# A fused two-layer graph kernel: the node pass's first six steps placed between the second edge stage's last groups

## What is computed

```python
h = relu(layernorm(x))
x = x + L0(h)     # edge messages (q*k*dk attention), summed by dst, times Wo, plus h
h = relu(layernorm(x))
x = x + L1(h)
# L1: deg = 1 + segment_sum(edge_weight, src); dinv = rsqrt(deg)
#     agg[i] = sum over edges src=i of dinv[i]*w*dinv[dst]*h[dst]  +  dinv[i]^2 * h[i]
#     out = relu(agg @ (W @ W1) + (b @ W1 + b1)) @ W2 + b2
```

## Time and profile before

| | before |
|---|---|
| median of 3 runs | 1825.09 us (1824.55 to 1827.22) |
| the profiled execution: its time | 1813.87 us |
| the profiled execution: span from first to last instruction | 1812.2 us |
| mean granted TensorE clock over the span | 0.943 |
| PE busy | 1607.8 us (89%) |
| DVE busy | 1424.0 us (79%) |
| POOL busy | 1214.8 us (67%) |
| ACT busy | 1127.9 us (62%) |

### The profile page before, as it was taken

One profiled execution on the slowest core, in us unless ns is written; L12 is line 12 of the kernel. 1 busy time (PEld: TensorE's weight loads), 2 busy tenths in 40 slices (PEclk: granted clock), 3 DMA queues, 4 the chain that ended last, 5 costly groups with the idle time before them and its releaser, 6 DMA issues.

```text
span 1812.2 us, 29106 instructions
## 1 busy us (share of the span) xinstructions
PE 1607.8 (89%) x6406; PEld 1097.8 (61%) x6406; DVE 1424.0 (79%) x5625; ACT 1127.9 (62%) x2142; POOL 1214.8 (67%) x864
## 2 busy tenths in 40 slices
PE   6999999999999927677675099999999999999998
PEld 3556666666666615455553066677666666666776
DVE  8887877777777539888785788888888888888873
ACT  2345566666666402222222398889998889888884
POOL 5325888888887457888887766666666666666650
PEclk9999999999999968888887599999999999999999
DMA  9999666666666736656655889999999999999971
GB/s 373 417 416 342 158 188 195 191 183 184 184 192 194 206 73 117 116 127 112 128 110 107 201 222 268 265 272 271 266 272 265 273 264 271 267 264 270 274 223 77
DMA packets 148029, 398.73 MB, mean 220 GB/s; under 512 B 20144, under 2 KB 56756, under 8 KB 147974
## 3 DMA queue, kind: packets, MB, share of 16 engines
q1 hardware_dynamic: 88038, 278.61, 44.5%
q0 software_dynamic: 56416, 115.46, 33.8%
q10 hardware_dynamic: 3520, 4.07, 0.7%
HBM read 217.84 MB, written 180.23 MB: 220 GB/s over the span
## 4 chain that ended last, share of the span: by engine, by line
PE 53%; POOL 20%; DMA 11%; DVE 9%; issue 6%; SPq 1%; ACT 0%; POOLq 0%; DVEq 0%; ACTq 0%
PE bank L1394 11%; PE bank L1383 11%; POOL sums_dram L504 9%; PE bank L1278 8%; DMA out_dram<-cg 6%; PE bank L1271 4%; PE bank L1285 4%; PE bank L1320 4%; POOL kept L601 4%; POOL cg L508 4%; POOL b_rs L500 3%; PE bank L1373 3%; DMA sums_dram<-ub,sidx 2%; PE bank L1259 2%; DVE cg L995 2%
## 5 line engine op out<-in xcount | busy, mean ns | idle before, releaser
L1394 PE MATMUL bank<-w_sb,kept 128*128 128x256 f32 x1568 | 354.3, 379 | 0.0
L1383 PE MATMUL bank<-kept,w 128*128 128x512 f32 x784 | 353.3, 593 | 0.0
L601 POOL TENSOR_TENSOR kept<-kept 128x1024 f32<-128x1024 f32 x98 | 232.3, 2370 | 177.1 <-DVE cg L995 177.1
L1394 PEld LDWEIGHTS bank<-w_sb,kept 128*128 128x128 f32 x1568 | 298.1, 190 | 81.7 <-issue 46.3
L1347 PE MATMUL bank<-cg,en 128*128 128x256 f32 x386 | 130.4, 482 | 121.7 <-ACT cg L1148 67.1
L500 POOL TENSOR_TENSOR b_rs<-b_ve,minus_half 128x8 f32<-128x8 f32 x102 | 210.3, 2062 | 28.2 <-DVE b_ve L1012 28.2
L1383 PEld LDWEIGHTS bank<-kept,w 128*128 128x128 f32 x784 | 141.8, 191 | 140.9 <-issue 140.9
L1186 ACT ACTIVATE kept<-kept,b_nb,b_rs 128x256 f32<-128x256 f32 x392 | 202.2, 588 | 22.0 <-DVE b_nb L985 22.0
L1176 ACT ACTIVATE kept<-kept,b_nb,b_rs 128x256 f32<-128x256 f32 x392 | 202.3, 589 | 10.2 <-DVE b_nb L985 10.2
L504 POOL DMA_INDIRECT sums_dram<-ub,sidx x96 | 156.2, 1627 | 53.8 <-issue 27.0
L1347 PEld LDWEIGHTS bank<-cg,en 128*128 128x128 f32 x386 | 93.0, 248 | 153.8 <-issue 136.7
(11 more groups left out here) (179 smaller groups left out, 3355.8 us busy)
## 6 DMA issues: line engine op xcount, KB each, us to landing
sums_dram<-cg SPq DMA_DIRECT2D x196, 512.0 KB, 15.2
kept<-in_x_dram SPq DMA_DIRECT2D x97, 512.0 KB, 6.0
kept<-sums_dram POOLq DMA_DIRECT2D x97, 512.0 KB, 10.0
cg<-sums_dram SPq DMA_DIRECT2D x97, 512.0 KB, 8.5
out_dram<-cg SPq DMA_DIRECT2D x97, 512.0 KB, 10.0
row_k<-keys_dram SPq DMA_DIRECT2D x24, 256.0 KB, 4.5
row_s<-in_src_dram SPq DMA_DIRECT2D x24, 256.0 KB, 4.3
row_d<-in_dst_dram SPq DMA_DIRECT2D x41, 128.0 KB, 3.9
```

The source lines that it names most:

```text
L601: pool.tensor_tensor(X1[k.slot(8)], X[k.slot(4)], H[k.slot(2)], ALU.add).then_inc(g_xh, 1)
L1383: ins = pe.matmul(bank[:, 2 + m, :], w01[:, c, m * P:(m + 1) * P], hT[k.slot(2)][:, c * GN:(c + 1) * GN], start=(c == 0), stop=(c == KC - 1))
L1394: ins = pe.matmul(to, rT[k.slot(2)][:, c * GN + j * P:c * GN + (j + 1) * P], w2_sb[:, c, :], start=False, stop=(c == KC - 1), skip_group_c ...
```

## The change

`AHEAD` becomes 6. VectorE, ScalarE and SP run `messages2` (SP: its row loads) for steps 0 to 11 as before (`first_quads`: four in line, eight in a loop), then 12 to 26 in line, and behind steps 13, 15, 17, 19, 21 and 23 they run node steps 0 to 5. POOL, all in line, runs node steps 0 to 5 behind its steps 14, 16, 18, 20, 22 and 24 (`lag=1`). PE has nothing to do in these node steps and runs `messages2(25)` and then node step 6 on.

In the first six node steps the sum X1 = X + H, which occurs in steps 2 to 5, is done on VectorE in four instructions of 128x256 instead of on POOL in one of 128x1024; POOL keeps the accumulating DMA and the power. The buffers over `kept` are ordered X, H, X1, H1, AG, hT, rT. Instead of one wait for 22 groups, SP waits for 4 groups ahead of its first X load, VectorE for the group over which each X1 lies (7 to 10) and, ahead of the first AG, for 18. SP's node step 6 loads X(6) and then S1(0) and S1(1), the first after the wait for all scatters. The memset of b_mv on VectorE comes behind step 11. All that follows node step 5 is as before.

```diff
@@ -26,7 +26,9 @@
 Q = 4
 NQ = -(-EC // Q)
 SPARE = ROWS - N
-AHEAD = 5
+AHEAD = 6
+FRONT_FROM = 12
+FRONT_AT = (13, 15, 17, 19, 21, 23)
 HOT_STEPS = (10, 8, 8, 8, 11, 11, 11, 11, 10, 10)
 HOT_RING = 6
 SCATTER_LAG = 9
@@ -302,10 +304,16 @@
             return place(late, [P, width])
 
         X = [part(G * D) for _ in range(4)]
-        X1 = [part(G * D) for _ in range(8)]
+        x_rooms = late[0] // (Q * D)
         H = [part(G * D) for _ in range(2)]
+        X1, x1_rooms = [], []
+        for _ in range(8):
+            X1.append(part(G * D))
+            x1_rooms.append(late[0] // (Q * D))
         H1 = [part(G * D) for _ in range(2)]
         AG = [part(G * D) for _ in range(2)]
+        ag_rooms = late[0] // (Q * D)
+        assert G == Q and ag_rooms <= NQ - 2
         hT = [part(KC * GN) for _ in range(2)]
         rT = [part(KC * GN) for _ in range(2)]
         ROOMS = -(-late[0] // D)
@@ -347,14 +355,21 @@
 
             return t[(slice(None), bass.ds(k.value(0, Q), chunks(k)), *i)]
 
-        def last_quads(messages2, nodes):
-
-            for i in range(AHEAD):
-                if i == 0:
-                    messages2(Step(NQ))
-                if i == 2:
-                    messages2(Step(NQ + 1))
-                nodes(Step(i))
+        def first_quads(eng, messages2):
+
+            for p in range(4):
+                messages2(Step(p))
+            with eng.Fori(1, FRONT_FROM // 4) as reg:
+                for u in range(4):
+                    messages2(Step(u, reg, 4))
+
+        def last_quads(messages2, nodes, since=FRONT_FROM, lag=0):
+
+            for p in range(since, NQ + 2):
+                messages2(Step(p))
+                for i in range(AHEAD):
+                    if FRONT_AT[i] + lag == p:
+                        nodes(Step(i))
 
         def load_pair(eng, k):
 
@@ -433,10 +448,8 @@
                                  src[bass.ds(k.value(0, Q * P), wide)].rearrange("(a e) -> a e", a=1)
                                  .broadcast_to([P, wide])).then_inc(n_row[k.slot(2)], 16)
 
-            run_steps(sp, NQ, 0, 4, 4, load_src)
-
-
-            sp.wait_ge(n_h, ROOMS // Q)
+            first_quads(sp, load_src)
+
             STORE = NODE_STEPS + 1
 
             def nodes(s):
@@ -445,17 +458,20 @@
                     if k.past(4):
 
                         pass_on(sp, (g_xh, k.value(-3)))
+                    elif not k.past(1):
+                        sp.wait_ge(n_h, x_rooms)
                     sp.dma_start(X[k.slot(4)][0:parts_of(k), :], group(x, k, parts_of(k))
                                  ).then_inc(g_x[k.slot(4)], 16)
-                k = s.back(5)
-                if k.within(NG):
-                    if not k.past(1):
-
-                        sp.wait_ge(n_sc, 16 * EC)
-                    if k.past(4):
-                        pass_on(sp, (g_ag, k.value(-3)))
-                    sp.dma_start(S1[k.slot(4)][0:parts_of(k), :], group(sums1, k, parts_of(k))
-                                 ).then_inc(g_s1[k.slot(4)], 16)
+                if s.past(AHEAD):
+                    for k in [s.back(5)] if s.past(AHEAD + 1) else [Step(0), Step(1)]:
+                        if k.within(NG):
+                            if not k.past(1):
+
+                                sp.wait_ge(n_sc, 16 * EC)
+                            if k.past(4):
+                                pass_on(sp, (g_ag, k.value(-3)))
+                            sp.dma_start(S1[k.slot(4)][0:parts_of(k), :], group(sums1, k, parts_of(k))
+                                         ).then_inc(g_s1[k.slot(4)], 16)
                 k = s.back(STORE)
                 if k.within(NG):
 
@@ -463,7 +479,8 @@
                     sp.dma_start(group(out, k, parts_of(k)), OUT[k.slot(2)][0:parts_of(k), :]
                                  ).then_inc(g_out[k.slot(2)], 16)
 
-            run_steps(sp, NG, STORE + 1, 8, 4, nodes)
+            last_quads(load_src, nodes)
+            run_steps(sp, NG, STORE + 1, 8, 4, nodes, start=AHEAD)
             for q in range(2):
                 sp.wait_ge(g_out[q], 16 * ((NG - q + 1) // 2))
 
@@ -587,18 +604,16 @@
                     for i in range(chunks(Step(k))):
                         scatter_add(sums1, sidx2[k % 4][:, i:i + 1], UB2[k % 2][i // 2][:, i % 2, :], last_row1, n_sc)
 
-            for p in range(NQ):
-                messages2(Step(p))
-
             def nodes(s):
                 k = s.back(2)
                 if k.within(NG):
 
-                    pass_on(pool, (g_h, k.value(1)))
-                    if k.past(8):
-
-                        pass_on(pool, (g_fin, k.value(-7)))
-                    pool.tensor_tensor(X1[k.slot(8)], X[k.slot(4)], H[k.slot(2)], ALU.add).then_inc(g_xh, 1)
+                    if s.past(AHEAD):
+                        pass_on(pool, (g_h, k.value(1)))
+                        if k.past(8):
+
+                            pass_on(pool, (g_fin, k.value(-7)))
+                        pool.tensor_tensor(X1[k.slot(8)], X[k.slot(4)], H[k.slot(2)], ALU.add).then_inc(g_xh, 1)
                     pass_on(pool, (g_xh, k.value(1)))
                     pool.dma_start(X1[k.slot(8)][0:parts_of(k), :], group(sums0, k, parts_of(k)),
                                    accum_op=ALU.add).then_inc(g_s0[k.slot(4)], 16)
@@ -609,7 +624,7 @@
                         pool.wait_ge(g_h1, k.value(-5))
                     inv_sqrt(b_ve[k.slot(2)][:, :, :], b_rs[k.slot(2)][:, :, :], g_ve, g_rs, k)
 
-            last_quads(messages2, nodes)
+            last_quads(messages2, nodes, since=0, lag=1)
             run_steps(pool, NG, NODE_STEPS, 8, 4, nodes, start=AHEAD)
 
 
@@ -966,7 +981,7 @@
                     dve.scalar_tensor_tensor(nb[q][:, 0:n, :], mv[q][:, 0:n, 0:1], -1.0, rs[q][:, 0:n, :], ALU.mult,
                                              ALU.mult).then_inc(n_nb, 1)
 
-            run_steps(dve, NQ, 0, 4, 4, messages2)
+            first_quads(dve, messages2)
 
             for i in range(2):
 
@@ -975,6 +990,16 @@
             def nodes(s):
                 a, v, r, t = s, s.back(1), s.back(5), s.back(4)
                 z = v.slot(2)
+                k = s.back(2)
+                if k.within(NG) and not s.past(AHEAD):
+
+                    dve.wait_ge(n_h, x1_rooms[k.slot(8)])
+                    dve.wait_ge(g_h, k.value(1))
+                    for j in range(G):
+                        at0 = slice(j * D, (j + 1) * D)
+                        ins = dve.tensor_tensor(X1[k.slot(8)][:, at0], X[k.slot(4)][:, at0], H[k.slot(2)][:, at0],
+                                                ALU.add)
+                    ins.then_inc(g_xh, 1)
                 if v.within(NG + 4):
                     dve.wait_ge(g_rs, v.value(1))
                     if r.within(NG):
@@ -1016,6 +1041,8 @@
                     dve.wait_ge(g_h1, k.value(1))
                     if k.past(2):
                         dve.wait_ge(g_T, k.value(-1))
+                    elif not k.past(1):
+                        dve.wait_ge(n_h, ag_rooms)
 
                     dve.wait_ge(g_s1[k.slot(4)], k.turns(4))
                     for j in range(G):
@@ -1156,7 +1183,7 @@
                         ins = act.activation(UB2[q][i].rearrange("p i d -> p (i d)"), bank[:, 6 * q + i, :], ACT.Copy)
                     ins.then_inc(n_UB, 1)
 
-            run_steps(act, NQ, 0, 4, 4, messages2)
+            first_quads(act, messages2)
 
             def nodes(s):
                 k = s.back(7)
@@ -1361,7 +1388,7 @@
                 ins.then_inc(g_bits, 1)
 
             def nodes(s):
-                if s.reg is None and s.off == AHEAD - 1:
+                if s.reg is None and s.off == AHEAD:
                     open_banks()
                 k = s.back(7)
                 if k.within(NG):
@@ -1395,7 +1422,7 @@
                                             start=False, stop=(c == KC - 1), skip_group_check=True)
                     ins.then_inc(g_m2, 1)
 
-            last_quads(messages2, nodes)
+            messages2(Step(NQ))
             run_steps(pe, NG, NODE_STEPS, 8, 4, nodes, start=AHEAD)
 
 
```

## The result

The changed kernel takes 1816.41 us (median of 5 runs, 1815.92 to 1819.55) against 1825.09 of before: ratio 0.9957, 95% interval 0.9942 to 0.9972. It is faster by 7.8 us by the ratio, 8.7 by the medians; 16.0 were forecast. The time lies inside the range and the sign is right, but the gain is about half of the forecast, so the sum is wrong somewhere.

The account below looks back on a forecast made before the run. POOL was taken to bound the edge stage, TensorE the node pass. With +15.5, -2.3 and -2.6 to the last scatter and a shorter way on, PE's full step moves from 1048.5 to 1032.5: 1825.1 - 16.0 = 1809.1 us, range 1802 to 1820.

Parts of the forecast that it names:

- POOL bounds the edge stage: Second edge stage: POOL is never free, so whatever is put into its queue there, the stage pays.
- the way from the last scatter to the first transposes: Hole before the node pass: last scatter ends at 1008.7, first transposes at 1019.0 us, against 998.10 and 1032.56 before.
- VectorE's lag is covered: Edge stage: VectorE's lag of up to 5.0 us per node step lies within 9.7 us of cover, costed at nothing.
- the rival: Edge stage: VectorE and POOL wait for one another in each node step, 46 us more, 1855 us; chance 6%.
- the 3.11 us wait between the last groups: POOL between the scatters of groups 22 and 23: hides node step 5, only 0.4 of its 3.5 us shows.
- the landing of group 23: POOL before group 24's scatters: a landing of 3.1 us replaces node steps 0 and 1 at 5.7, so -2.6.
- The price of the node steps on POOL, 15.5: POOL's edge stage: powers at 2.3 us, DMAs at 1.2, step 5 mostly hidden; +15.5 us, between 13 and 17.
- Spreads the loads, one in two groups: -2.3, at worst 0: Edge stage: POOL's wait of 2.33 us behind the burst of X loads goes, as the loads are spread.
- AG(1) follows AG(0) by VectorE's own work: From first transposes to PE's full step: AG(1) 5.5 us behind AG(0), the whole way 13.5 instead of 16.0.
- The rate of the node pass can't change by this edit: its loop is untouched: Node pass behind PE's full step: a PE-bound constant, no change.
- waits for room: The waits for n_h are 15 groups overdue when they come, AG's overdue too: cost nothing.
- it waits for nobody: POOL in the edge stage before the change: only issues scatters and gathers, with 0.3 us of issue each.

Follow-up runs that it names:

- X1 sums on POOL: Changed kernel with the X1 sums of node steps 2 to 5 put back on POOL inside the edge stage; ratio 1.0018 to the kernel before.
- six-group run: Changed kernel with the six node steps behind steps 18 to 23, one in each group instead of one in two; ratio 1.0019 to the kernel before.
- the thin: Changed kernel with the loads of X(0) to X(5) fetching 16 of 1024 columns, output partly wrong; ratio 0.9920 to the kernel before.
- held loads: Changed kernel with each edge-stage X load, all bytes kept, waiting until PE has finished a group; ratio 0.9927 to the kernel before.
- X(7) early: Changed kernel with SP issuing the load of X(7) with X(6), ahead of its wait for the scatters; ratio 0.9940 to the kernel before.
- the run with the loop elsewhere: Changed kernel with VectorE's node loop begun at step 24 instead of 16, eight more steps in line; ratio 0.9927 to the kernel before.

## Why the prediction was half wrong

**Right.** That POOL bounds the edge stage (X1 sums on POOL: four of them, 11.1 us). That the way from the last scatter to the first transposes shrinks by 24 us: 25.3 (34.5 to 9.2). That VectorE's lag is covered (no wait of POOL for UB or statistics), and what happens where it isn't: the rival was put at 46 us more in all, and the six-group run showed 13 (a rival's price that was much too high; which of the cover and the gather waits took the rest was not tried). That the 3.11 us wait between the last groups hides node step 5 (3.06 us stand there now), that the burst's wait of 2.3 us goes, and that the landing of group 23 takes 3.1 (3.3 at 1020.30).

**The price of the node steps on POOL, 15.5, was too high.** They cost 1.6 or 1.9 each for a power and 2.6 with the DMA: 11.3 for five, and the sixth nothing. I took the record of the power (2.1) for its time on the path. This was 4 us in the change's favour.

**"Spreads the loads, one in two groups: -2.3, at worst 0" was the step that failed on the edge stage.** I saw that a burst of X loads makes the scatters ahead of it land late, and then took a single load as free. SP lets each go as a group's last scatter is issued, so each delays their landing: three waits of 1.5 to 2.3 us and smaller ones, 6 us by the thin and by the held loads. This was the largest single term. Together the edge stage grew by 13.5 us (335.5 to 349.0) where I had 10.6: 3 us lost.

**"AG(1) follows AG(0) by VectorE's own work" failed on X(7).** I named X(6) ahead of the wait for the scatters, but not X(7) behind it in SP's queue, though what X(7) itself needs was there long before. The way to the full step stayed at 16.1 instead of 13.5: 2.6 us lost; with X(7) early it is 12.5.

**"The rate of the node pass can't change by this edit: its loop is untouched" was the step that failed behind it.** I put this term at nothing, and it is 5 us (D 757.9 to 763.0; 759.0 to 764.0 in the first pair), 3.0 to 4.4 of them at VectorE's stall. The loop's instructions are the same, but the code ahead of it is not, and its entry stalls. By the run with the loop elsewhere the stall is worth 6 us of the time, give or take 3; why the entry stalls stays open. Sum: 335.5 + 34.5 + 15.9 = 385.9 before and 349.0 + 9.2 + 16.1 = 374.3 after is 11.6 of gain at the full step instead of 16.0; less 5.1 in the node pass, 6.5; the ratios of the two comparisons say 7 to 8.

**Two readings that were wrong and cost nothing.** The waits for room were called 15 groups overdue. By the change's own numbers they are about 8 to 12: X needs 4 groups where 12 are done, the X1 need 7 to 10 where 16 to 22 are. And "it waits for nobody" left out eight waits of 0.3 us in which a gather of POOL followed a scatter's landing: a sign that the landings were covered, but not by much.

## What to carry to other kernels

When work is moved under the end of a stage, count what each moved DMA delays at the moment at which its queue will let it go: a load that left together with scatters whose landing was waited for 6.7 us later was paid by that waiter, and the same load some 10 us later, with 11 us to go, was free. In an in-order queue look at what stands behind the stage's last wait, not only ahead of it. And after any edit that changes the straight code ahead of an aligned loop, look for "issue" time at the loop's first instruction: here an untouched loop lost at its entry a good part of what was won before it.

## What the runs showed of the hardware

VectorE stood still for 4.1 to 5.5 us at the entry of an aligned loop (the kernel asks for the place of its first instruction by `addr_align`, and the padding ahead of it is jumped over), once in each of the seven profiles in which the six node steps are moved and the loop begins at step 16; it did not in the two of before, whose code ahead of that entry is shorter, nor in the three with the loop begun at step 24, whose code ahead of it is longer. Running through the padding took 10.1 us. The Trainium skill ("Runtime: NRT & Kernel Launch", Instruction fetch mechanics) states that a taken branch whose target is not in the current two-page window forces the target page to be fetched before execution goes on. A stall at the entry that comes and goes with the code ahead of it fits that, but no run here shows a fetch, or which page the target lay in.

A stop of PE of 2.9 us was followed by products of 4.88 us instead of 3.60, and a granted clock of 0.83 over 10 us. That is a mean over both levels: in windows of 1 us the clock is 1.00 (2.4 GHz) through the stop, 0.50 (1.2 GHz) from 1115 to 1118 us and 1.00 again from 1119. The two rounds lost 4.8 us together. A gap does not always cost more than its length: after the stop of 2.17 us in the changed kernel's second profile the clock stayed at 1.00 and the products at 3.60, while after one of 2.15 us in the run with the X1 sums on POOL it stood at 0.50 from 1134 to 1136 us.

AG(0), four instructions with two inputs each in SBUF, took 3.24 us beside POOL's X1 sum (1029.62 to 1032.86 against 1028.72 to 1031.37), against 1.67 without. And when a load of 512 KB left with a group's last scatter, POOL waited 1.5 to 2.3 us for their landing behind four gathers, which without it covered the landing.
